# Moving one relation's weights-times-vectors work behind the last attention head

## The reference

```
x = layernorm(x + GAT(x))        # 8 heads of 768, then 1 head
x = layernorm(x + RGAT(x))       # 3 relations, 4 heads, then 1 head
x = layernorm(x + RGCN(x))       # 4 relations, 3 layers
x = layernorm(x + GCN(x))        # 2 layers
```

## Time and profile before

| | |
|---|---|
| median of the runs | 1947.81 us |
| profiled execution, its own time | 1949.55 us |
| its span | 1947.8 us |
| TensorE (PE) busy | 1809.3 us, 93% |
| VectorE (DVE) busy | 1236.8 us, 63% |
| ScalarE (ACT) busy | 720.1 us, 37% |
| GpSimd (POOL) busy | 697.6 us, 36% |
| mean granted TensorE clock | 0.959 |

### The profile page before, as it was taken

How to read it: one execution, slowest core, us unless ns; L and a number is a source line. 1 busy time by engine, 2 the same in 40 slices (tenths; PEclk the granted TensorE clock), 3 DMA queues, 4 the chain that set the end, 5 groups by cost and what they waited for, 6 DMA issues and landing times. The chain is left out here.

```text
span 1947.8 us, 26928 instructions
## 1 busy us (share of the span) xinstructions
PE 1809.3 (93%) x8997; PEld 1512.9 (78%) x8997; DVE 1236.8 (63%) x2166; ACT 720.1 (37%) x1159; POOL 697.6 (36%) x386
## 2 busy tenths in 40 slices
PE   8999898999999999879988798979999999999797
PEld 3444585999999998768966588977777888899776
DVE  9998476878887886667547856664324232453635
ACT  0203634445444444422466634313224223332221
POOL 1666231323323422212776655402233332423311
PEclk9999999999999999979989899979999999999989
DMA  1002632222212321112410022122222222323320
GB/s 20 18 4 75 243 113 81 73 66 90 89 50 88 101 67 59 49 46 102 136 49 1 1 76 71 49 95 61 71 77 81 79 88 72 92 85 101 96 91 33
DMA packets 54199, 143.08 MB, mean 73 GB/s; under 512 B 13780, under 2 KB 13908, under 8 KB 53076
## 3 DMA queue, kind: packets, MB, share of 16 engines
q1 hardware_dynamic: 46898, 107.15, 17.9%
q10 hardware_dynamic: 7202, 34.63, 5.0%
HBM read 129.18 MB, written 12.58 MB: 73 GB/s over the span
## 5 line engine op out<-in xcount | busy, mean ns | idle before, releaser
L737 POOL TENSOR_TENSOR w_pair<-early,w_pair 128x768 fp32r<-128x768 f32 x234 | 445.3, 1932 | 921.1 <-ACT w_pair L1314 921.0
L795 PE MATMUL ps<-w_pair,cols_x 128*128 128x384 f32 x2088 | 376.6, 337 | 0.6 <-DVE al_part L1708 0.6
L795 PEld LDWEIGHTS ps<-w_pair,cols_x 128*128 128x128 f32 x2088 | 363.8, 189 | 5.5 <-issue 2.8
L795 PE MATMUL ps<-w_pair,wide 128*128 128x384 f32 x1872 | 335.3, 339 | 13.1 <-DVE wide L1699 11.7
L795 PEld LDWEIGHTS ps<-w_pair,wide 128*128 128x128 f32 x1872 | 330.8, 191 | 17.5 <-DVE wide L1699 13.0
L1314 ACT ACTIVATE w_pair<-early 128x768 fp32r<-128x768 f32 x234 | 181.4, 840 | 350.5 <-PE ps L795 156.3
L1260 PE MATMUL ps<-wide,w_pair 128*128 128x512 f32 x972 | 226.4, 392 | 2.2 <-DVE wide L1699 2.2
L1260 PEld LDWEIGHTS ps<-wide,w_pair 128*128 128x128 f32 x972 | 182.6, 189 | 40.1 <-DVE wide L1699 2.6
L428 PE MATMUL count_ps<-early,src_hot 128*128 (+1 forms) x816 | 179.9, 383 | 7.7 <-DVE early L348 7.6
L428 PEld LDWEIGHTS count_ps<-early,src_hot 128*128 (+1 forms) x816 | 80.3, 98 | 106.8 <-issue 10.3
L1228 PE MATMUL ps<-prob,wide 128*128 128x512 f32 x588 | 152.5, 400 | 0.0
(11 more groups left out here) (252 smaller groups left out, 2450.1 us busy)
## 6 DMA issues: line engine op xcount, KB each, us to landing
early<-weights SPq DMA_DIRECT2D x240, 384.0 KB, 3.1
multi<-attn ACTq DMA_DIRECT2D x9, 768.0 KB, 4.6
edge_mask<-counts ACTq DMA_DIRECT2D x13, 512.0 KB, 3.3
kept<-early ACTq DMA_DIRECT2D x3, 1536.0 KB, 6.0
multi<-kept ACTq DMA_DIRECT2D x3, 1536.0 KB, 6.8
counts<-out SPq DMA_DIRECT2D x8, 512.0 KB, 2.6
src_hot<-weights SPq DMA_DIRECT2D x10, 384.0 KB, 6.7
edge_mask<-masks ACTq DMA_DIRECT2D x6, 512.0 KB, 3.6
```

The lines of the kernel that those rows point to most:

```text
L737: return nc.gpsimd.tensor_tensor(dst, whole, high.bitcast(F32), ALU.subtract)
L795: mm = nc.tensor.matmul(ps[:, m, 0:HW], left[:, a, k, m * P:(m + 1) * P], w_pair[:, slot_of[0], b, k, :], start=(k == 0 and a + b == 0), s ...
```

## The change

Only relation 0 stays in counting (`EARLY_R = 1`). Relation 1 takes the place of relation 2 in the first head (`HEAD_R = 1`). Relation 2 (`LAST_R = 2`) is done behind the last head, its groups put between the small steps there; its six pieces are loaded by SP, between passes 29 and 30, into memory that `cols_x` no longer needs. The two result items of a relational head are parted: the first stays behind s = 5, the second goes behind s = 8. Around this the end of counting, the start of the layers and the first head are arranged anew.

```diff
@@ count_and_weigh, SP: pieces 2 to 5 are all loaded ahead of x
-                    for i in range(2, 8):
+                    for i in range(2, EARLY_R * WT_PIECES):
                         load_piece(sp, i)
                     sp.dma_start(acc, x).then_inc(res_in, 16)
-                    for i in range(8, EARLY_R * WT_PIECES):
-                        load_piece(sp, i)
@@ the flag is stored ahead of the last mask
+                if r == 3:
+                    sp.wait_ge(flag_ready, 1)
+                    sp.dma_start(flag, flag_i[:]).then_inc(stored, 16)
@@ ScalarE
             copy_weights(8, 9)
+            copy_attention_weights(0)
             ... four copies of mask 1
-            copy_weights(9, 14)
+            act.wait_ge(wk_turned, 1)
+            copy(wkq[:, :, 0, 0:8 * EARLY_R], ...).then_inc(wkq_hi, 1)
             act.wait_ge(c_ready, NB)
             copy(out16[:, 2], rel_c[:]).then_inc(out16_ready, 1)
-            copy_weights(14, EARLY_R * WT_GROUPS)
-            ...
@@ VectorE: the flag's two operations move between rel_c and has_edge
+            dve.wait_ge(most_turned, 1)
+            step(nc.vector.tensor_reduce(most_row[:], ...))
+            nc.vector.tensor_scalar(flag_i[:], ...).then_inc(flag_ready, 1)
@@ TensorE, behind the loop over 9 groups (18 before)
+            pe.wait_ge(flag_ready, 1)
+            turn_mask(1)
+            turn_mask(2)
             ... six transposes of wk_rows (twelve before)
+            turn_mask(3)
@@ graph_layers, SP
+            sp.dma_start(b_cols[:], bias_cols).then_inc(small_in, 16)
+            ... flag_sb, vec, count16[0], mask: the five loads that ScalarE issued
             for j in range(1, 4):
                 load_pass(j)
             ... pieces 0 to 3
             load_pass(4)
+            load_pass(5)
             ... pieces 4 and 5
-            with sp.Fori(5, PASSES) as j:
+            with sp.Fori(6, 30) as j:
+                load_pass(j)
+            sp.wait_ge(prod_done, 4 * 26)
+            for i in range(WT_PIECES):
+                _, t, n = piece_at(i)
+                sp.dma_start(last_raw[:, i], weights[32 + 2 * LAST_R + n, t]).then_inc(last_in, 16)
+            with sp.Fori(30, PASSES) as j:
                 load_pass(j)
@@ GpSimd: the identity matrix of counting is kept, two operations go
-            nc.gpsimd.memset(ident[:], 0.0).then_inc(consts, 1)
-            nc.gpsimd.affine_select(out=ident[:], ...)
@@ TensorE: turn(0) no longer waits for the constants
-            pe.wait_ge(consts, 5)
             pe.wait_ge(res_in, 16)
             turn(0)
@@ TensorE, behind the last head
+            pe.wait_ge(last_in, 16 * WT_PIECES)
+            turn_last(0)
+            turn_last(1)
+            pe.wait_ge(acc_added, 70)
+            weigh_last(0)
+            turn_last(2)
             pe.wait_ge(kc_ready, 9)
             turn_source()
+            weigh_last(1)
+            turn_last(3)
             pe.wait_ge(q_ready, 17)
             spread_source()
+            for g in range(2, 5):
+                weigh_last(g)
+                turn_last(g + 2)
             pe.wait_ge(uv_ready, 9)
             turn_small(uvc[:, 0, 0], 4)
+            weigh_last(5)
+            turn_last(7)
             pe.wait_ge(q_ready, 18)
             spread_uv()
+            weigh_last(6)
+            turn_last(8)
+            weigh_last(7)
+            weigh_last(8)
+            def turn_last_weights():
+                pe.wait_ge(wk_hi, 2)
+                ... six transposes of 8 rows, then wk_turned
             pe.wait_ge(rows_split, NB)
-            row_sums(rows[0], prob, 80, acc_added, 69, 0)
+            pe.wait_ge(wk_hi, 2)
+            row_sums(rows[0], prob, 80, acc_added, 69, 0, {2: turn_last_weights})
@@ ScalarE, first head
                         if u == 0:
                             copy_rows(h * 5 + 1, 2)
+                            if not with_last:
+                                split_high(j_rows + 1, 1)
-                        copy_weights(0, 2)
-                    split_high(j_rows + 3, 1)
-                    if not with_last:
-                        copy_weights(2, 4)
+                        copy_weights(0, 4)
@@ ... and behind the loop over exponentials, ahead of wk_row
+                    split_high(j_rows + 3, 1)
@@ ScalarE, behind the last head
+            copy_weights(0, 2, WT_GROUPS)
             copy_rows(41, 2)
+            copy_weights(2, 7, WT_GROUPS)
             copy_rows(43, 4)
+            copy_weights(7, 8, WT_GROUPS)
             copy_v(44)
             for s in range(NB + 1):
                 ... exponential
+                if s == 0:
+                    copy_weights(8, 9, WT_GROUPS)
                 ... high
+                if s == 2:
+                    act.wait_ge(wk_done, 2)
+                    copy(hv_rows[0:8, :], ...).then_inc(wk_hi, 1)
+            act.wait_ge(wk_turned, 2)
+            copy(wkq[:, :, 0, 8 * LAST_R:], last_cols).then_inc(wkq_ready, 1)
             ... act.wait_ge(x_lo, 84), then the loads of the bias row and of the residual
@@ VectorE, ahead of add_bias_to_residual(0)
+            dve.wait_ge(wkq_ready, 3)
+            sub(wkq[:, :, 1, 8 * LAST_R:], ...).then_inc(wkq_ready, 1)
@@ relational_items
-            if h and s == 5:
-                items += [(h - 1, None, 0), (h - 1, None, 1)]
+            if h and s in (5, 8):
+                items.append((h - 1, None, s // 8))
```

More of the change, by code:

```diff
@@ L66, in early_loads @@
     hidden_bias = ctx.enter_context(nc.sbuf_tensor("hidden_bias", [P, 3, KB], F32))
-    return {"early": (early, raw_in, res_in), "wkq": wkq, "kq_cols": kq_cols, "hidden_bias": hidden_bias}
+    ident = ctx.enter_context(nc.sbuf_tensor("ident", [P, P], F32))
+    return {"early": (early, raw_in, res_in), "ident": ident, "wkq": wkq, "kq_cols": kq_cols, "hidden_bias": hidden_bias}
 def split_early(early):
@@ L79 @@
 WT_GROUPS = 3 * WT_PIECES // 2
-EARLY_R = 2
+EARLY_R = 1
+HEAD_R = 1
+LAST_R = 2
 def piece_at(i):
@@ L490, in _ @@
                     weigh_weights(g - 1)
[L491 to L496, removed]
-                    pe.wait_ge(most_ready, 1)
-                    pe.wait_ge(mask_dve, NB + 1)
-                    nc.tensor.transpose(ps[0:1, 1, 0, 0:P], most[:], ident_f[:]).then_inc(turned, 1)
+                if g == 2:
+                    pe.wait_ge(most_ready, 1)
+                    pe.wait_ge(mask_act, 1)
+                    nc.tensor.transpose(ps[0:1, 1, 0, 0:P], most[:], ident_f[:]).then_inc(most_turned, 1)
+            pe.wait_ge(flag_ready, 1)
+            turn_mask(1)
+            turn_mask(2)
             for r in range(EARLY_R):
@@ L519, in tile_at @@
 def tile_at(h, s):
-    return W_AT + 12 * h + s + 2 * max(h - 1, 0) + (2 if h and s > 5 else 0)
+    return W_AT + 12 * h + s + 2 * max(h - 1, 0) + (1 if h and s > 5 else 0) + (1 if h and s > 8 else 0)
 def relational_items():
@@ L549, in sem @@
             return ctx.enter_context(nc.semaphore(name))
+        with nc.sbuf_tensor("last_raw", [P, WT_PIECES, 2, HW], F32) as last_raw:
+            pass
         cols_x = sb("cols_x", [P, 2, KB, N], F32R)
@@ L709, in load_piece @@
                     sp.wait_ge(wt_turned, (3 * (i - 4) + 2) // 2 + 1)
-                sp.dma_start(acc_flat[:, 768 * (i % 4):768 * (i % 4 + 1)], weights[32 + 2 * EARLY_R + n, t]).then_inc(wt_in[i % 4], 16)
+                sp.dma_start(acc_flat[:, 768 * (i % 4):768 * (i % 4 + 1)], weights[32 + 2 * HEAD_R + n, t]).then_inc(wt_in[i % 4], 16)
+            sp.dma_start(b_cols[:], bias_cols).then_inc(small_in, 16)
+            sp.dma_start(flag_sb[:], flag).then_inc(small_in, 16)
+            sp.dma_start(vec, attn0[0:1].partition_broadcast(P)).then_inc(vec_in, 16)
+            sp.dma_start(count16[0], counts[TOTAL]).then_inc(cnt_in, 16)
+            sp.dma_start(mask[:], masks[0]).then_inc(mask_in, 16)
             for j in range(1, 4):
@@ L1368, in turn @@
                     copy(cols_x[:, 0, f, :], ps[:, 4 + f % 4, :]).then_inc(turn_hi, 1)
-            act.dma_start(b_cols[:], bias_cols).then_inc(small_in, 16)
-            act.dma_start(flag_sb[:], flag).then_inc(small_in, 16)
-            act.dma_start(vec, attn0[0:1].partition_broadcast(P)).then_inc(vec_in, 16)
-            act.dma_start(count16[0], counts[TOTAL]).then_inc(cnt_in, 16)
-            act.dma_start(mask[:], masks[0]).then_inc(mask_in, 16)
             split_high(0, 0, wait=False)
@@ L1377, in _, with copy_weights @@
             split_high(1, 1, wait=False)
-            def copy_weights(first, end):
+            def copy_weights(first, end, base=0):
                 for g in range(first, end):
-                    act.wait_ge(wt_turned, g + 1)
+                    act.wait_ge(wt_turned, base + g + 1)
                     copy(wt_cols[g % 2], ps[:, 4 + g % 2, :]).then_inc(wt_copied, 1)
@@ L1397, in head @@
                             copy_v(h * 5 + 4)
-                    if not with_last:
-                        copy_weights(0, 2)
```

(16 more changed lines are left out.)

54 lines of the change are left out of this document (29 added, 25 removed).

## The result

The changed kernel takes 1942.99 us (median of 10 runs, 1932.68 to 1944.78), the kernel before 1948.82 in the same session (10 runs, 1946.78 to 1949.99): a ratio of 0.9965, interval [0.9953, 0.9978]. So it is faster by 5.8 us, a third of the 18.4 us forecast, and it lies above the range of 1919 to 1942.

A forecast was written before the change was run, and what follows sets the result against it. TensorE, busy 93% of the span, was taken to set the end nearly always, so its gaps decide. Terms -6.4 - 2.1 - 5 - 6.5 + 12.2 - 10.6 = -18.4 us gave 1929.5 us, range 1919 to 1942.

The forecast's parts named there:

- End of counting, start of the layers: Two terms before the heads: gain 6.4 us (4 to 8) with SP last, then gain 2.1 (1 to 3.5).
- First head: Two terms there: gain 5 us (2 to 6.5) in the first half, 6.5 (4.5 to 8) in the groups.
- What is late next: First head, groups: the split ahead slips ScalarE's copy of the 8 rows by 1.7 us, leaving 6.5 of 8.2.
- moved low parts: First head: GpSimd's 5.8 us of low parts, moved, fall on VectorE's first tile of the next head, taking 4.3 us.
- Nine groups go: End of counting: nine groups of about 1.55 us leave, 14 us of TensorE; the term's gain is 6.4 us.
- Behind the last head: Nine groups added there; the residual's load is issued late behind the third source step: loss 12.2 us (3.5 to 17).
- Rival A: Behind the last head: the residual isn't late, the tail costs only the filling, about 4 us: 1921; chance 0.12.
- C: Rival: the tail behind the last head stays at 1.2 GHz, a loss of 38 us: 1955; chance 0.06.
- Relational heads: Parting the result items shortens three TensorE waits: 3.2, 4.8 and 2.6 us, gain 10.6 (4 to 14).
- by the second item it is ahead again: Relational heads: VectorE, at 1.5 to 1.7 us a tile against TensorE's 2.27, leaves only 0.3 to 0.5 us of wait.
- rival B: Relational heads: parted items gain nothing, a second wait of 3 us behind s = 8 cools TensorE: 1940; chance 0.10.
- Rival D: Early gains: SP's stores or the first low parts are later, half is lost: 1937; chance 0.12.

The follow-up runs named there:

- run 1: Changed kernel with ScalarE issuing the bias row and the residual's load ahead of its wait for the turned weight rows behind the last head: 1934.08 us, ratio 0.9927.
- run 2: Changed kernel with the two result items of a relational head together again behind the sixth tile: 1944.77 us, ratio 0.9984 to the kernel before.
- run 4: Changed kernel with ScalarE's copy of the 8 weight rows in the first head ahead of its split of the next weights: 1941.76 us, ratio 0.997.
- run 6: Changed kernel with the second result item of a relational head behind the tenth tile (s = 9) instead of the ninth: 1935.04 us, ratio 0.9942.
- run 7: Run 6 with TensorE's transposes of the next u and v ahead of a group's third tile instead of the second: 1934.87 us, ratio 0.9932.
- run 5: Kernel before with the rearranged first head alone, TensorE's program unchanged: 1934.52 us, ratio 0.9928 to the kernel before.
- run 3: Changed kernel with 60 tiny unread transposes added on TensorE at the end of counting, moving the loop's place: 1937.04 us, ratio 0.9945.
- run 9: Run 3 with 20 and with 130 transposes instead of 60, one execution each: 1934.85 us and 1946.0 us.

## Why the prediction was wrong

**End of counting, start of the layers:** right, 12.4 us in this trace instead of 8.5. Most of the excess belongs to this one execution. ScalarE's copy of the ninth group starts at 203.35 in it instead of 205.71, where I had left it, and the layers' loads at 218.85. In the profiles of runs 1, 2, 4, 6 and 7, whose program is the same up to there, the copy starts at 204.9 to 206.2 and the loads at 220.4 to 221.7; my working had 221.4. SP was the last engine, as said.

**First head:** right. 11.5 us forecast, 11.5 in the trace, 14.3 as a change by itself (run 5). "What is late next", the copy of the 8 rows, came where I had put it. Its price was 3.7 us instead of 1.7, since I had counted the delay and not the slow clock behind it. Of the moved low parts: VectorE's first two dot products beside them take 2.20 and 2.19 us and the later ones 0.55, as before. Each of the two has about the length of one of GpSimd's three operations (6.07 us together), and that agrees with the Trainium skill, *SBUF — State Buffer*, section "SBUF: two separate sides", by which the engine that comes second on the shared port pair waits for the other's whole instruction. The tile took 4.9 us, 4.3 forecast. That the half still came out at 6.2 instead of 5 has another reason: of the three small operations behind the masked maximum only two were slow beside the low parts of pass 4 (1.47 and 1.77 us) and the third took 0.16; before, all three were (1.65, 1.77, 1.77).

**Heads 1 to 7: the missing term.** The sum had nothing for this stretch, where the diff doesn't touch a line. It cost 8.2 us in the trace, of which 5.1 are the two gaps and some 2.5 the cold matmuls behind the first; run 3 got 6.0 of it back. The step that failed is the first sentence on the end of counting, "Nine groups go": I counted their time and not that they and six transposes, 78 matmuls in all, move the loop over the heads in TensorE's program, and the sum put the heads at 0.

**Behind the last head:** right, 12.4 for 12.2, and the mechanism was the one given: run 1 isolates it. Rival A (the load isn't late) is refuted, and so is C: the groups ran at a granted clock of 1.00 from 834 to 851. That the number fits to 0.2 us is in part luck. I had said 1.00 for the row sums too, but the clock fell, to 0.57 at 855 to 862, behind a stretch in which TensorE was busy half of the time and then waited 2.01 us; up to the six transposes they took 12.8 us instead of 9.8. This delayed the load, which is issued behind them. Against it, the row sums began 1.5 us earlier than I had worked out, and the second half took 10.16 us instead of some 11.1.

**Relational heads: the step that failed** was "by the second item it is ahead again, and I find only 0.3 to 0.5 us of wait there". It gained 1.5 us in the trace and 1.8 in run 2, not 10.6. I followed VectorE's pace past the second item and left out ScalarE's order: TensorE's spread (L1111) waits for a copy of v that ScalarE makes behind a tile's high part, and the item now stood ahead of both. My own rival B (nothing gained, a second wait of 3 us behind s = 8, GpSimd close to TensorE's pace) was near the truth in these heads. It had the engine wrong in the first two, where that wait, 1.96 and 2.01 us, is for the copy, and right in the third, where it is 2.45 us for GpSimd (0.81 in run 1, whose edit doesn't touch these heads: this one varies). By what ends them, the 14.5 us of gaps are 7.5 for GpSimd, 4.0 for the copy and 3.0 for VectorE. With the item one tile later (run 6) the copy's gaps are gone and the third head's last is 0.83, and the forecast nearly holds: 7.8 us of 10.6 by the traces, of which 1.6 may be that variation.

Two errors of 8 and 9 us on one side, then, and 3.9 us of larger gains on the other. The range was too narrow since all its bounds came from stretches that the diff names. (Rival D's 1937 doesn't follow from its own words: half of the four early gains, 20.0 us, is 10.0, and the time 1939.4. No chance or bound hangs on it.)

## What to carry to other kernels

When instructions are taken out ahead of a long loop, look at the loop's first gap in each round and at the instruction queue's packets, before and after: a handful of idle instructions in a wait can be worth more than the edit. When an item is moved between tiles, follow each engine's program past it, the small copies too; the wait sits at whichever small operation was queued behind its new place. And time the parts of a bundled change alone: here one of them was worth more than twice the bundle.

## What the hardware showed that I had not expected

- The place of a loop in TensorE's program decides whether its instructions are fetched again at every round: 18 packets of about 16 KB more and two stalls of 2.0 to 3.0 us, some 6 us in all with the slow clock behind them. It stalled at places 130 matmuls apart and not at three places between (run 9). The profile calls such a stall "issue".
- Behind a gap of 1.01 us the granted clock was 0.50 from 298 to 300 (without the gap, in run 4, 1.00), whereas in the relational heads the six matmuls behind gaps of 1.49 and 1.00 us took 1.53 and 1.56 us, and those behind the next gap, 1.96, took 2.51.
- Adding 5.07 us of TensorE work in an idle stretch made the kernel 6.0 us faster.
